# Expert layer with the projection weights standing in TensorE and 512 tokens moving past them, the group weights multiplied in by GpSimd

## What is computed

```python
x = hidden_states.reshape(-1, H)                    # after a layernorm
scores = softmax(x @ gate_w.T)                      # N x 64
topk_w, topk_idx = top_k(scores, 8)
w_e = zeros((N, 64)).at[arange(N)[:, None], topk_idx].add(topk_w)
flat = w_e[:, inv_map]                              # N x 8 groups x 8
scalar = flat.sum(-1)                               # the weight of a group for a token
soft = softmax(where(flat == 0, -1e9, flat), -1)
xg = x[:, None, :] + einsum('ngi,ghi->ngh', soft, mask_up_w)
g = einsum('ngh,gih->ngi', xg, gate_proj_w)
u = einsum('ngh,gih->ngi', xg, up_proj_w)
d = einsum('ngi,ghi->ngh', silu(g) * u, down_proj_w)
y = einsum('ng,ngh->nh', scalar, d)
```

## Time and profile before

| | |
|---|---|
| timed runs, median of 3 | 1656.84 us |
| the profiled execution's own time | 1660.86 us |
| its span | 1658.8 us |
| mean granted TensorE clock | 0.988 |
| start of the block `ffn` | 1160.8 us |
| TensorE busy in the span | 94% |
| DVE, ACT, POOL busy in the span | 71%, 49%, 49% |

### The profile page before, as it was taken

How to read it: one execution, slowest core, us unless ns; L and a number is a source line. 1 busy time by engine, 2 the same in 40 slices (tenths; PEclk the granted TensorE clock), 3 DMA queues, 4 the chain that set the end, 5 groups by cost and what they waited for, 6 DMA issues and landing times. The chain is left out here.

```text
span 1658.8 us, 69237 instructions
## 1 busy us (share of the span) xinstructions
PE 1565.8 (94%) x30224; PEld 1343.1 (81%) x30224; DVE 1181.2 (71%) x2780; ACT 814.4 (49%) x1902; POOL 806.3 (49%) x673
## 2 busy tenths in 40 slices
PE   5689999999999999999999999997999999999998
PEld 4568878877778777877877878875899999999998
DVE  6778878887788778878877888886645446445443
ACT  6555555555556555555555555543433333333332
POOL 4376767676667666676767676762010010011000
PEclk9889999999999999999999999998999999999999
DMA  9523221112231112222112311112100000000000
GB/s 299 130 71 79 55 54 45 52 41 73 72 77 53 48 51 77 64 64 73 55 45 63 93 42 42 45 39 77 59 27 1 26 27 1 26 27 1 13 14 13
DMA packets 83981, 91.87 MB, mean 55 GB/s; under 512 B 33696, under 2 KB 58272, under 8 KB 83680
## 3 DMA queue, kind: packets, MB, share of 16 engines
q1 hardware_dynamic: 83680, 87.44, 18.5%
HBM read 55.67 MB, written 14.94 MB: 43 GB/s over the span
## 5 line engine op out<-in xcount | busy, mean ns | idle before, releaser
L1395 ACT ACTIVATE probs<-aps,nmax 128x896 f32<-128x896 f32 (+7 forms) x512 | 378.1, 740 | 410.3 <-DVE nmax L1443 398.4
L1443 DVE CUSTOM_DVE_ANT_0 aps<-aps,mask_row 128x896 f32<-128x896 f32 (+7 forms) x512 | 380.7, 759 | 122.9 <-PE aps L46 119.4
L46 PE MATMUL aps<-kTh,qh 128*128 128x512 f32 (+3 forms) x768 | 291.2, 379 | 13.7 <-DVE ql L1131 7.2
L1122 POOL TENSOR_TENSOR rot<-rot,sinT 64x512 f32<-64x512 f32 x126 | 160.4, 1273 | 292.7 <-DMA rot<-rot 292.7
L46 PE MATMUL aps<-pT_second,vrep 32*64 32x128 f32 (+1 forms) x15616 | 263.5, 260 | 26.2 <-issue 23.3
L46 PEld LDWEIGHTS aps<-pT_second,vrep 32*64 32x64 f32 x15616 | 224.8, 131 | 66.1 <-issue 53.7
L1453 DVE STREAM_TRANSPOSE pT_second<-probs 128x896 f32<-128x896 f32 (+3 forms) x256 | 264.0, 1032 | 4.7 <-ACT probs L1395 4.5
L46 PE MATMUL aps<-kTl,qh 128*128 128x512 f32 (+3 forms) x768 | 259.2, 345 | 1.6 <-issue 1.6
L46 PE MATMUL aps<-kTh,ql 128*128 128x512 f32 (+3 forms) x768 | 223.2, 345 | 0.0
L46 PEld LDWEIGHTS aps<-kTh,qh 128*128 128x128 f32 x768 | 145.5, 189 | 75.0 <-issue 38.9
L1826 DVE TENSOR_TENSOR aTl<-fps,aTh 128x512 fp32r<-128x512 f32 (+1 forms) x96 | 61.9, 646 | 167.3 <-ACT aTh L1769 167.3
(11 more groups left out here) (195 smaller groups left out, 3032.9 us busy)
## 6 DMA issues: line engine op xcount, KB each, us to landing
rot<-rot SPq DMA_DIRECT2D x256, 64.0 KB, 2.5
linv_b<-inverses_scratch SPq DMA_DIRECT2D x128, 128.0 KB
wqs<-wq_scratch SPq DMA_DIRECT2D x30, 256.0 KB, 3.6
raw_numbers<-in_x SPq DMA_DIRECT2D x8, 512.0 KB, 6.4
vrep<-values_scratch SPq DMA_DIRECT2D x16, 256.0 KB, 4.6
inverses_scratch<-linv_t SPq DMA_DIRECT2D x256, 1.0 KB
acc<-in_x SPq DMA_DIRECT2D x16, 256.0 KB, 3.2
x_scratch<-acc SPq DMA_DIRECT2D x16, 256.0 KB, 3.1
```

Source lines behind the costliest of these rows:

```text
L46: return nc.tensor.matmul(out, lhsT, rhs, start=start, stop=stop, skip_group_check=True)
L1122: eng.tensor_tensor(rot2[:, k, :], rot2[:, k, :], t.sinT[:, cols], ALU.mult).then_inc(q_turned, 1)
L1395: nc.scalar.activation(probs[:, SLOT[x, r], 0:w], sps[:, at:at + w], ACT.Exp, bias=nmax[:, c, a, j:j + 1], scale=-1.0, accum_out=lsum[:, c ...
L1443: nc.vector.tensor_tensor_reduce(out=s, in0=s, in1=mask[:, N - PW[c][j]:N], scale=-1.0, scalar=3.0e38, op0=ALU.add, op1=ALU.min, accum_out ...
```

## The change

`gate_up` is turned round. The columns of gate and up are laid out anew as 11 blocks of 128 (`MEMBERS`; `DIMS` lists which column of which group stands where: a group has 176, so blocks 4, 5 and 10 are mixed from three or four groups). For a block m and a half of 512 tokens, `products` has 128 x 128 of the weights standing in TensorE and moves the 512 tokens: 6 matmuls for gate, 6 for up. The result has the columns on the partitions, which is how `down` needs it, so there are no `transposes`. `soft` becomes one matmul of 128 rows and 512 columns for each of gate and up, with `mw` spread into zeroed blocks in the place of the keys (`mwz`); block 5 needs two. The program walks through 88 steps (8 halves x 11 blocks) instead of 32 tiles x 8 groups, and `down` follows two steps behind.

Since a token is now a column, its group weight is no longer one number per partition. DVE turns `mass` with a 128 x 32 transpose, `keep_mass` writes it to DRAM, and `spread_mass` reads it back once per block with a DMA that gives every partition of a member the row of its group (18 DMAs for a half, 2.75 MB). GpSimd multiplies the Silu by it (`weigh`). The preparation of the mask term is cut to the places of the new layout: 7 and 11 small operations on ACT and DVE instead of 1 and 2.

```diff
-            def gate_up(i, g):
-                n = i * G + g
+            def products(n, u):
+                H, m = divmod(n, MC)
...
+                if n >= 2:
+                    pe.wait_ge((silu_done, act_done)[u], n - 1)
                 for k in range(KC):
-                    for j, (x, w) in enumerate(((t.xTh, wth), (t.xTh, wtl), (t.xTl, wth))):
-                        mm(nc, banks[:, n % GB, 0:GU], x[:, k, tok_of(i)], columns(w, g, k), k == 0 and j == 0, False)
+                    for j, (x, w) in enumerate(((t.xTh, t.wth), (t.xTh, t.wtl), (t.xTl, t.wth))):
+                        mm(nc, banks[:, 2 * (n % 2) + u, :], columns(w, m, k, u), x[:, k, tok(H)], k == 0 and j == 0, False)
...
+        PE_AT = {0: 2, 1: 3, 2: 4, 3: 6, 4: 7, 5: 9, 6: 10}
+        ACT_AT = {0: 2, 1: 3, 2: 5, 3: 6, 4: 8, 5: 9, 6: 10}
+        DVE_AT = {0: 0, 1: 2, 2: 3, 3: 4, 4: 5, 5: 5, 6: 7, 7: 8}
...
+            def gate(n):
+                dve.wait_ge(up_ps, n + 1)
+                dve.wait_ge(weighted, n + 1)
...
+            def high(n):
+                act.wait_ge(act_done, n + 1)
...
+            def low(n):
+                dve.wait_ge(aT_h, n + 1)
...
+            def weigh(n):
+                H, m = divmod(n, MC)
+                pool.wait_ge(silu_done, n + 1)
+                pool.wait_ge(mass_loaded[m], 16 * len(MEMBERS[m]) * (H + 1))
+                nc.gpsimd.tensor_tensor(sg[:, n % SLOTS, :], sg[:, n % SLOTS, :], mass_b[:, m, :], ALU.mult)\
+                    .then_inc(weighted, 1)
...
-            for H in range(2, HALVES):
-                router_root(nc, t, H)
-                pool.wait_ge(t.xT_ps, 2 * H)
-                for i in range(HT):
-                    router_norm(nc, t, H, i)
+            for n in range(TOTAL):
+                H, m = divmod(n, MC)
+                weigh(n)
+                if m in (0, 1) and 0 < H < HALVES - 1:
+                    if m == 0:
+                        router_root(nc, t, H + 1)
+                        pool.wait_ge(t.xT_ps, 2 * H + 2)
+                    for i in range(2 * m, 2 * m + 2):
+                        router_norm(nc, t, H + 1, i)
...
+            sp.wait_ge(t.mass_kept, 64)
+            for m in range(4):
+                spread_mass(0, m)
             load(2)
-
             sp.wait_ge(t.x2_stored, 64 * B)
             sp.dma_start(raw_d[:], ins["down"].rearrange("(m p) d -> p m d", p=P)).then_inc(down_loaded, 16)
```

More of the change, by code:

```diff
@@ L29 @@
 GU = 2 * I
+GB = 2 * P
 QC = 512
@@ L616, in mask_products @@
     for n, (k, part) in enumerate([(k, part) for k in range(KC) for part in (t.wth, t.wtl)]):
[L617 to L620, removed]
+        for g, m, rows, first, width in mask_places(q):
+            last = mm(nc, mask_part(bank, g, rows, first, width), t.mu4[:, k, g, :],
+                      both_columns(part, m, k, rows).bitcast(F32), n == 0 and width == P, n == 3)
@@ L621, in mask_products, with mask_clear @@
     last.then_inc(t.mw_ps, 1)
+def mask_clear(nc, t, q):
+    nc.gpsimd.memset(t.kTh[:, q, :].bitcast(F32), 0.0).then_inc(t.mw_zero, 1)
+    nc.gpsimd.memset(t.kTl[:, q, 0:2 * GB].bitcast(F32), 0.0).then_inc(t.mw_zero, 1)
 def mask_high(nc, t, q, bank):
     nc.scalar.wait_ge(t.mw_ps, q + 1)
-    nc.scalar.copy(t.mwh[:, q, :], bank[:, 0:GU]).then_inc(t.mw_h, 1)
+    for g, m, rows, first, width in mask_places(q):
+        row = slice(32 * (g % 4), 32 * (g % 4) + 32)
+        last = nc.scalar.activation(mask_part(t.mwh[:, q, :], g, rows, first, width),
+                                    mask_part(bank, g, rows, first, width), ACT.Copy, scale=t.hl_sign[row, 0:1])
+    last.then_inc(t.mw_h, 1)
@@ new lines, in parts @@
+            def parts(n):
+                H, m = divmod(n, MC)
+                for part, at in ACT_AT.items():
+                    if at == m and H + 1 < HALVES:
+                        router_scalar(nc, t, H + 1, part, r_bank)
+            second_quad_high()
+            router_scalar(nc, t, 0, 5, r_bank)
+            router_scalar(nc, t, 0, 6, r_bank)
+            for n in range(TOTAL):
+                silu(n)
+                if n == 0:
+                    down_high(0)
+                if n == 1:
+                    down_high(1)
+                    down_high(2)
+                if n > 0:
+                    high(n - 1)
+                if n == 3:
+                    mask_high(nc, t, 1, banks[:, 6, :])
+                parts(n)
@@ L1800, in _ @@
+            high(TOTAL - 1)
         @block.vector
@@ L1842, in _, with parts @@
+            def parts(n):
+                H, m = divmod(n, MC)
+                for part, at in DVE_AT.items():
+                    if at == m and H + 1 < HALVES and (H > 0 or part > 0):
+                        router_vector(nc, t, H + 1, part, r_bank)
             router_vector(nc, t, 0, 7, None)
             second_quad_low()
[L1844 to L1862 removed]
@@ L1863, in _ @@
-            last = TILES - 1
-            low(last, 1)
-            low(last, 2)
-            add_up(last)
+            for n in range(TOTAL):
+                gate(n)
+                if n == 0:
+                    down_low(0)
+                if n > 0:
+                    low(n - 1)
+                if n == 1:
+                    down_low(1)
+                    down_low(2)
+                if n == 4:
+                    mask_low(nc, t, 1, banks[:, 6, :])
+                parts(n)
+                if n % MC == LAG - 1 and n > MC:
+                    add_up(n // MC - 1)
@@ L1868, in _ @@
+            low(TOTAL - 1)
+            add_up(HALVES - 1)
         @block.gpsimd
```

426 lines of the change are left out of this document (199 added, 227 removed).

## The result

The changed kernel takes 1667.65 us, the median of 6 runs (1664.47 to 1673.58), where the kernel before took 1658.01 in the same comparison (6 runs, 1655.88 to 1664.16). The ratio is 1.006 with a 95% interval of 1.0041 to 1.0078: slower by 0.6%. The forecast was 1649.0, faster; the time lies 4.65 us above the range. The profiled execution took 1669.44 us with a span of 1667.7; that of before had 1660.86 and 1658.8. So the spans differ by +8.9 us where the sum said -7.8.

What follows compares the result with a forecast made beforehand. TensorE's moved columns were taken as the bound. Terms -36.7 - 6.0 + 17.1 + 7.0 + 1.0 + 2.8 + 6.0 + 1.0 = -7.8 us took the median from 1656.84 to 1649.0 us; range 1627 to 1663.

Steps and rivals of the forecast that it cites:

- Part 1: TensorE's steady work in the expert block: steps of 4.67 us, a gain of 36.7 us over eight halves (27 to 45).
- Part 3: Router norms from GpSimd reach TensorE late: a wait of 2.85 us in six halves, +17.1 us (13 to 25).
- Part 4: DVE's router operations beside GpSimd's multiplications: `rot` in block 9 +7.0 us (0 to 9), selection in block 5 +1 (0 to 3).
- Part 6: Start of the expert block: `raw_down` behind spread DMAs, later first Silu, longer mask products; +6.0 us (2 to 12).
- Rival C: No gain: 512-column matmuls cost 0.24 us or more, or the start loses 12 us; 1657 us, chance 0.12.
- Part 2: TensorE's waits for `aTl` in the expert block go: -6.0 us (0 to -6).
- Rival B: DVE and GpSimd block each other throughout, at low parts and router chains in blocks 5 and 8; 1664 us, chance 0.18.
- Part 5: End of the attention: mask term in seven ACT and seven DVE operations delays last sums and barrier; +2.8 us (1 to 5).
- Part 7: Kernel's end: `add_up` follows the last matmul with four additions instead of one; +1.0 us.

Runs made afterwards that it cites:

- e6: Changed kernel, with GpSimd's multiplications in blocks 6 and 9 waiting until DVE finishes the router's selection and inner softmax: 1658.67 us, 0.9999 of before.
- e3: Changed kernel, with TensorE's router parts moved behind `down` and DVE's `add_up` ahead of block 1's gate product: 1644.45 us, 0.991 of before.
- e4: Changed kernel, with the multiplication by the group weights moved from GpSimd to DVE: 1637.52 us, 0.9869 of before.
- e2: Changed kernel, with only block 0's weights spread ahead of the load of the down weights at the start: 1663.03 us, 1.0021 of before.
- e1: Changed kernel, with DVE's last two attention sums ahead of the mask term's small operations: 1661.09 us, 1.0018 of before.
- e5: Changed kernel, with group weights spread for the first half only and used for all eight: 1670.6 us, 1.007 of before.
- e7: Changed kernel with the three edits of e4, e1 and e2 together: 1631.41 us, 0.9829 of before.
- e8: e7 with e3's edit on top, router parts behind `down`: 1631.29 us, 0.9833 of before.

## Why the prediction was wrong

Its direction failed. The sum's large terms, parts 1 and 3, were right in kind and nearly in size. Part 4 and part 6 were too small by half, the clock was no term at all, and all three pointed the same way.

**Part 1, right.** 4.70 us for a step against 4.67; on 88 steps 2.6 us of 36.7. Rival C's first half, a dearer 512, does not hold: 0.2335 us beside the 0.232 of the earlier trace rows.

**Part 2, right outside the start.** After the first half there is one wait for `aTl`, of 0.4 us, near the end. The 5.4 us of the first half are in part 6.

**Part 3, right in kind and a little too large.** Six waits, 14.6 us by the loads of weights and 11.9 by the matmuls, against 17.1. The chain ran as laid out: 1.5 us from the root to the first norm, two norms in 2.44 us (1.22 each), the multiplication in 1.29, two norms in 2.49:

```profile
1309.53 2.44 POOL L894 TENSOR_SCALAR cosT<-x,f_aggr,f_rstd 128x256 f32<-128x256 f32 x2 [0.18 <-POOL f_rstd L887]
...
1313.21 2.49 POOL L894 TENSOR_SCALAR cosT<-x,f_aggr,f_rstd 128x256 f32<-128x256 f32 x2
```

The last two were not slowed to 1.85, the value taken for one of them.

**Part 4, the step that failed.** For `rot` 1.0 us a time was forecast and 1.27 came. For the selection in block 5 and 6 the words were "ready at 8.4 where TensorE asks at 8.4; I put +1 for all halves (0 to 3)". It was 8.0 us, 1.14 each time: 16.9 us for the two where the sum had 8.0, and e6 shows that 13.1 of the 16.9 are DVE held up by GpSimd. The chain itself was placed right: block 5 of half 6 begins at 1574.96, so the subtraction, begun at 1582.96 and free of GpSimd 0.42 us long, would have been ready at 8.4. What the step left out is GpSimd's multiplication of block 6, which the sum lays out for block 9 and not here. Set like that one, behind the gate's products of block 6 (from 5.1 to 6.75) and Silu, it falls on about 7.5 to 8.8, on top of the subtraction; that is my estimate from the rows of the prediction, and the trace has 7.7 to 9.0. A chain that ends just when TensorE asks, beside an instruction that can hold it up for 1.3 us, is no near zero: it should have stood with half of that price or as a rival. Rival B spoke of whole instructions of 1.285 us lost in blocks 5 and 8. It named the right mechanism and put it at the low parts too, where the trace shows none (681 ns each, where the earlier trace rows has 690). Its time, 1664, is 3.65 us from the result, and it had 0.18. That nearness is partly luck: the low parts that it priced did not lose anything, and the start and the clock, which it left as they were, did.

The Trainium skill (SBUF — State Buffer, "Who interferes with whom") says that in this contention the order of issue decides who blocks. By that rule a wait that lets DVE issue first is enough, and e6 agrees: 1209 ns became 425.

**The clock, a term that was not in the sum.** Waits of 2.85 us at the norms and 3 at the start were forecast, and nothing was put down for the clock behind them. Two falls of 1.5 us came in the halves 1 to 6, 3.0 us, and about 2 us more at the start, where the clock stands at half behind the wait for `raw_down`:

```profile
1180.00:1184.00 4.00, 0.00 (x0) 0.00 (x0) 2.02 (x3) 3.96 (x7) 1.84 (x2) 0.71 0.86 242
1184.00:1188.00 4.00, 3.36 (x14) 3.29 (x15) 4.00 (x4) 1.03 (x2) 1.63 (x1) 0.50 0.05 16
```

**Part 5, too small.** +4.4 by the wait at the barrier (+4.1 by the block's start) instead of +2.8, inside its bounds of 1 to 5. The seven pieces take ACT 2.91 us and DVE 1.97 + 0.92 = 2.89, where the terms meant 1.85 (0.45 + 1.4; its own prices for seven pieces add up to 1.71) and 4 x 0.4 + 3 x 0.23 = 2.3. The "7 and 11 small operations" of the section on the change are the pieces of the two mask terms: 7 on each of the two engines here, 11 on each in the block.

```profile
1155.31 2.91 ACT L662 ACTIVATE mwh<-aps,hl_sign 32x256 fp32r<-32x256 f32 x7 [5.70 <-PE aps L47]
...
1158.25 1.97 DVE L675 SCALAR_TENSOR_TENSOR kTh<-aps,hl_sign,mwh 32x256 fp32r<-32x256 f32 x4 [4.75 <-ACT mwh L662]
1160.23 0.92 DVE L675 SCALAR_TENSOR_TENSOR kTl<-aps,hl_sign,mwh 32x96 fp32r<-32x96 f32 x3
```

On ACT a piece of 256 costs 0.465 us and the narrow ones from 0.305, where 0.3 and 0.17 were taken; on DVE 0.48 and 0.305 against 0.4 and 0.23. Small pieces don't shrink with their width as I let them. All of ACT's by their durations (ns, least, median, most):

```profile
L662 ACT ACTIVATE mwh<-aps,hl_sign x7: 305/465/468, 1155.3 to 1157.9; 32x256 fp32r<-32x256 f32 x4, 32x96 fp32r<-32x96 f32 x2, 32x64 fp32r<-32x64 f32 x1
```

**Part 6, too small by about half.** The first half lost 7.8 us more than its terms, of which this part was 6.0. TensorE stood 5.4 us for the first `down` instead of 3: `raw_down` landed 12.2 us after its issue, with 14 more spread DMAs issued right behind it as well as the 1 MB ahead,

```profile
1167.48 0.51 SPq L1704 DMA_DIRECT2D raw_down<-in_down  x1
1168.03 10.47 SPq L1696 DMA_DIRECT2D mass_b<-mass_scratch  x14
```

The DMA share was 0.93 and 1.09 from 1164 to 1180 us, so the DMA engines were busy all that time. With it go 2 us of half clock, 0.7 of the selection's wait, which falls in this half as well, 0.3 for the longer steps and 0.8 where the router's first product waits for `ql`. That is 6.2 of the 7.8; the rest stays open. The small operations of the mask term (1.7 us) came as forecast.

**Part 7, a little too small.** From the start of the last matmul to the end it is 2.9 us before (1655.84 to 1658.8) and 4.5 after (1663.14 to 1667.7): +1.6 instead of +1.0.

In the six halves between, the waits as TensorE's weight loads count them exceed the forecast by 1.0 (selection) + 0.27 (`rot`) - 0.42 (norms), the steps by 0.33 and the clock by 0.5: 1.7 us a half, where 7.2 / 6 = 1.2 were lost. The loads wait in part while matmuls are still running, which may be why they add up to more; at the norms the matmuls count 11.9 us where the loads count 14.6.

What would have turned the forecast: part 4 with its true 8.0 and 8.9 us and part 6 with 11 instead of 6 give about +6, and the clock +3 more, which is +9 as measured. That it comes out so close is partly luck: the longer steps (+2.6), part 5 (+1.6) and part 7 (+0.6) are left out of it, and so are what part 3 had too much (-2.5) and the part of the waits that lies beside running matmuls.

## What to carry to other kernels

When work moves to an engine whose instructions can hold up another's, as GpSimd's multiplication held up DVE here, lay out every pair of instructions of the two within one of their durations of each other, and price a near tie at half the blocked instruction, not at nothing. A new stage that TensorE waits for costs its wait and, when the wait is over 2 us, sometimes a stretch of half clock behind it; ask first whether the waiting instruction can stand behind work that is ready (e3), or the late work on an engine with room (e4). And put the transfer that an engine waits for ahead of those that nobody waits for yet: their order in the queue was worth 3.8 us here.

## What the runs showed of the hardware

- A wait of TensorE of 2.2 us was followed by a stretch at half clock in some halves and not in others of the same execution (halves 1 to 6: two in the changed kernel and in e2, three in e1, e5 and e6; none in e3, e4, e7 and e8, where the matmuls' waits in these halves are 1.2 us at most), at 1.5 us each. What decides between them was not found.
- ACT loads a function's table ahead of the wait of the instruction that needs it: the load at 1579.88 was done 0.78 us before Silu began, and the loads for Silu behind the router's two Exps of each half ended 0.56 to 0.8 us before it. So this load of 1.28 us did not delay Silu here.
- An ACT piece of 32 partitions with 256 elements takes 0.465 us, one of 64 still 0.305: 2.91 us for seven, where one of 352 columns on all partitions took 0.45.
- A DMA that spreads a row of weights over its partitions takes SP about 0.75 us to issue at the start of the block (10.47 us for 14) and lands 4.3 us later (256 KB); 18 of them a half cost TensorE nothing once the start is over (e5).
- DVE's subtraction with two inputs in SBUF took 1209 ns when GpSimd's multiplication began 0.34 us before it (1582.62 and 1582.96), and 425 when the multiplication had to wait for it (e6); TensorE waited 13.1 us less by it. In e3 DVE was held up just as long, and TensorE did not wait at these places, because it asked later.
